# Expert loops of a two-layer gated block: one Sigmoid for SiLU, activations in PSUM, and the next rows converted before the last split

## What is computed

```python
# layer 0: experts with a squared ReLU, F = 256
inter = jnp.einsum('ecd,efd->ecf', binned, w1_stack)
inter = jnp.square(jax.nn.relu(inter))
outb = jnp.einsum('ecf,edf->ecd', inter, w2_stack)
...
# layer 1: experts with SiLU gating, D_FF = 512
g = jnp.einsum('nd,edf->nef', xf, gate_w) + gate_b
u = jnp.einsum('nd,edf->nef', xf, up_w) + up_b
h = jax.nn.silu(g) * u
expert_out = jnp.einsum('nef,efd->ned', h, down_w) + down_b
```

## Time and profile before

| what | before |
|---|---|
| median of 3 runs | 1481.43 us (1478.41 to 1485.65) |
| span of the profiled execution, first to last instruction | 1462.4 us |
| median less that span | 19.0 us |
| PE busy | 1092.1 us, 75% of the span |
| DVE busy | 790.0 us, 54% |
| ACT busy | 418.9 us, 29% |
| POOL busy | 362.7 us, 25% |
| mean granted PE clock | 0.872 of full speed |

### The profile page before, as it was taken

How to read it: one execution, slowest core, us unless ns; L and a number is a source line. 1 busy time by engine, 2 the same in 40 slices (tenths; PEclk the granted TensorE clock), 3 DMA queues, 4 the chain that set the end, 5 groups by cost and what they waited for, 6 DMA issues and landing times.

```text
span 1462.4 us, 16573 instructions
## 1 busy us (share of the span) xinstructions
PE 1092.1 (75%) x5562; PEld 904.4 (62%) x5562; DVE 790.0 (54%) x1774; ACT 418.9 (29%) x788; POOL 362.7 (25%) x294
## 2 busy tenths in 40 slices
PE   1978889787666663998999579898971488897850
PEld 1647666575565662786777458686860377897840
DVE  5456546656444436646565544535455466667633
ACT  1203121122132341233332332424220144453420
POOL 4204152131421351410101220101014322213225
PEclk9989989897888985999999679999985599998985
DMA  7600032000375650200000100000005544443435
GB/s 265 225 1 29 1 119 68 1 0 1 132 212 167 179 174 0 58 0 1 1 0 15 44 29 0 1 0 1 1 1 190 176 130 130 130 137 122 129 99 168
DMA packets 92431, 114.66 MB, mean 78 GB/s; under 512 B 6608, under 2 KB 77776, under 8 KB 92240
## 3 DMA queue, kind: packets, MB, share of 16 engines
q1 hardware_dynamic: 72480, 78.46, 16.5%
q0 software_dynamic: 19888, 35.40, 8.3%
HBM read 77.14 MB, written 36.70 MB: 78 GB/s over the span
## 4 chain that ended last, share of the span: by engine, by line
PE 53%; DVE 22%; issue 6%; POOL 6%; ACT 6%; DMA 5%; SPq 2%; DVEq 0%; POOLq 0%; ACTq 0%
PE PS L194 12%; PE PS L196 11%; PE PS L195 11%; PE PS L1577 7%; PE PS L1493 4%; DVE act L513 3%; PE PS L1468 3%; DMA xg<-routed 3%; POOL routed L759 2%; POOL HB L819 2%; POOL rstd L752 2%; PE PS L1389 1%; PE PS L1516 1%; DVE st L1036 1%; DVE SM L1310 1%
## 5 line engine op out<-in xcount | busy, mean ns | idle before, releaser
L752 POOL TENSOR_TENSOR rstd<-ve,minus_half 128x4 f32<-128x4 f32 x40 | 40.6, 1016 | 410.1 <-DVE ve L1043 251.6
L194 PE MATMUL PS<-xt,split 128*128 128x256 f32 x412 | 121.3, 295 | 10.9 <-issue 7.8
L194 PE MATMUL PS<-split,hs 128*128 128x256 f32 x244 | 84.2, 345 | 49.8 <-DVE hs L521 49.8
L195 PE MATMUL PS<-xt,split 128*128 128x256 f32 x412 | 119.3, 290 | 0.0
L196 PE MATMUL PS<-xt,split 128*128 128x256 f32 x412 | 118.9, 289 | 0.0
L1577 PE MATMUL PS<-VP,HB 128*128 128x257 f32 x384 | 97.0, 416 | 16.0 <-DVE VP L1322 16.0
L1577 PEld LDWEIGHTS PS<-VP,HB 128*128 128x128 f32 x384 | 80.1, 210 | 35.2 <-DVE VP L1322 21.8
L513 DVE SCALAR_TENSOR_TENSOR act<-act 128x256 f32<-128x256 f32 x84 | 70.8, 843 | 56.2 <-ACT act L481 56.2
L446 POOL TENSOR_TENSOR split<-raw,split 128x1024 fp32r<-128x1024 f32 (+1 forms) x15 | 66.5, 4432 | 138.4 <-DMA raw<-down_w 81.9
L194 PEld LDWEIGHTS PS<-xt,split 128*128 128x128 f32 x412 | 82.6, 200 | 14.4 <-issue 10.5
L194 PEld LDWEIGHTS PS<-split,hs 128*128 128x128 f32 x244 | 55.9, 229 | 57.1 <-DVE hs L521 57.1
(11 more groups left out here) (308 smaller groups left out, 2871.4 us busy)
## 6 DMA issues: line engine op xcount, KB each, us to landing
xg<-routed SPq DMA_DIRECT2D x44, 256.0 KB, 2.7
outputs<-y SPq DMA_DIRECT2D x40, 256.0 KB, 3.0
outputs<-zeros SPq DMA_DIRECT2D x3, 2048.0 KB, 16.1
routed<-zeros SPq DMA_DIRECT2D x20, 256.0 KB, 2.5
raw<-m_w SPq DMA_DIRECT2D x16, 256.0 KB, 5.9
split<-m_w POOLq DMA_DIRECT2D x16, 256.0 KB, 4.0
x_base<-X SPq DMA_DIRECT2D x8, 512.0 KB, 3.8
raw<-gate_w SPq DMA_DIRECT2D x8, 512.0 KB, 6.3
```

The costliest lines, as they stand in the source:

```text
L194: pe.matmul(out_, a[1], b[0], start=first, stop=False)
L195: pe.matmul(out_, a[0], b[1], start=False, stop=False)
L752: pool.tensor_tensor(rstd[h][:], ve[h][:], minus_half[:], ALU.pow).then_inc(sem("rstd_ready"), 1)
```

## The change

SiLU is made another way: ACT makes sigmoid(g + gate_b) in one instruction, and DVE makes `(g + gate_b) * sigmoid`, with g read from PSUM. The buffer `hbg` and its one instruction go. `h` is no longer in SBUF: it is written into the PSUM bank of its chunk, columns 256 to 511 (over the up product in stage 1, beside the product in stage 0), and both its parts are made from there. In stage 1 ACT's `x_hi` goes ahead of the last chunk's high part, and DVE's `x_lo` ahead of the last chunk's low part. SP reads the row number of the next load before it waits for the turned rows, and no longer after. The diff, cut:

```diff
         def group_in(sp, m, t):
             r = sp.value_load(table[m][0:1, bass.ds(t + 2 * E, 1)], min_val=0, max_val=XROWS - G)
+            if not isinstance(t, int):
+                counted(sp, m)
+                sp.wait_ge(sem(f"m{m}_turned"), t)
             sp.dma_start(moe[m].xg[:], routed[m][bass.ds(r, G), :].rearrange("(a p) d -> p a d", p=P)).then_inc(sem(f"m{m}_xg"), 16)
...
                 with sp.Fori(lo, hi) as t:
-                    counted(sp, m)
-                    sp.wait_ge(sem(f"m{m}_turned"), t + 2)
                     group_in(sp, m, t + 2)
...
+        def h_part(f):
+            return PS[:, f, G:2 * G]
...
+            def h_hi(t, f):
+                act.wait_ge(sem(f"m{m}_h"), t * w.fc + f + 1)
+                act.activation(w.hs[:, 0, f], h_part(f), ACT.Copy).then_inc(sem(f"m{m}_hhi"), 1)
...
-                            act.activation(w.act[:, f % 2, 0], PS[:, f, 0:G], ACT.Tanh, bias=hbg[:, b:b + 1], scale=0.5)
-                            act.activation(w.act[:, f % 2, 1], PS[:, f, 0:G], ACT.Identity, bias=hbg[:, b:b + 1], scale=0.5).then_inc(sem(f"m{m}_act"), 1)
+                            act.activation(w.act[:, f % 2, 0], PS[:, f, 0:G], ACT.Sigmoid, bias=col("gate_b", b)).then_inc(sem(f"m{m}_act"), 1)
...
+            def h_lo(t, f):
+                dve.wait_ge(sem(f"m{m}_h"), t * w.fc + f + 1)
+                dve.wait_ge(sem(f"m{m}_hhi"), t * w.fc + f + 1)
+                dve.tensor_tensor(w.hs[:, 1, f], h_part(f), w.hs[:, 0, f].bitcast(F32), ALU.subtract).then_inc(sem(f"m{m}_hlo"), 1)
...
-                            dve.scalar_tensor_tensor(out=w.h[:, f], in0=PS[:, f, 0:G], scalar=0.0, in1=a[:, 0],
+                            dve.scalar_tensor_tensor(out=h_part(f), in0=PS[:, f, 0:G], scalar=0.0, in1=a[:, 0],
                                                      op0=ALU.max, op1=ALU.mult).then_inc(sem(f"m{m}_h"), 1)
                         else:
-                            dve.scalar_tensor_tensor(out=a[:, 0], in0=a[:, 0], scalar=1.0, in1=a[:, 1],
-                                                     op0=ALU.add, op1=ALU.mult).then_inc(sem(f"m{m}_silu"), 1)
+                            dve.scalar_tensor_tensor(out=a[:, 1], in0=PS[:, f, 0:G], scalar=col("gate_b", e * w.fc + f),
+                                                     in1=a[:, 0], op0=ALU.add, op1=ALU.mult).then_inc(sem(f"m{m}_silu"), 1)
...
-                            dve.scalar_tensor_tensor(out=w.h[:, f], in0=PS[:, f, G:2 * G], scalar=col("up_b", e * w.fc + f),
-                                                     in1=a[:, 0], op0=ALU.add, op1=ALU.mult).then_inc(sem(f"m{m}_h"), 1)
+                            dve.scalar_tensor_tensor(out=h_part(f), in0=PS[:, f, G:2 * G], scalar=col("up_b", e * w.fc + f),
+                                                     in1=a[:, 1], op0=ALU.add, op1=ALU.mult).then_inc(sem(f"m{m}_h"), 1)
...
+                    if m == 0:
+                        h_lo(t, w.fc - 1)
+                        x_lo(t + 2)
+                    else:
+                        x_lo(t + 2)
+                        h_lo(t, w.fc - 1)
```

More of the change, by code:

```diff
@@ L155, in build @@
         rbf = [sb(f"rbf{h}", [P, 2, TT, E], BF16) for h in two]
-        ONCE = {"act": ("tanh_g", "hbq", "w3_hi", "ew", "gt_hi", "hbg"),
+        ONCE = {"act": ("tanh_g", "hbq", "w3_hi", "ew", "gt_hi"),
                 "dve": ("w3_split", "bb", "g1", "be1", "row_max", "wmax", "ewT", "gt_lo", "gbias"),
@@ L228, in moe_buffers @@
             w.act = sb(f"act{m}", [P, 2, w.ups, G], F32, st)
-            w.h = sb(f"h{m}", [P, w.fc, G], F32, st)
             w.hs = sb(f"hs{m}", [P, 2, w.fc, G], F32R, st)
@@ L269, in build @@
         DB = sb("DB", [P, E, D], F32, part_m[1])
-        hbg = sb("hbg", [P, E * F2 // P], F32, part_m[1])
         part_m[1].close()
@@ L479, in moe_act @@
                             b = e * w.fc + f
-                            act.activation(w.act[:, f % 2, 0], PS[:, f, 0:G], ACT.Tanh, bias=hbg[:, b:b + 1], scale=0.5)
-                            act.activation(w.act[:, f % 2, 1], PS[:, f, 0:G], ACT.Identity, bias=hbg[:, b:b + 1], scale=0.5).then_inc(sem(f"m{m}_act"), 1)
+                            act.activation(w.act[:, f % 2, 0], PS[:, f, 0:G], ACT.Sigmoid, bias=col("gate_b", b)).then_inc(sem(f"m{m}_act"), 1)
                             if f:
-                                act.wait_ge(sem(f"m{m}_h"), t * w.fc + f)
-                                act.activation(w.hs[:, 0, f - 1], w.h[:, f - 1], ACT.Copy).then_inc(sem(f"m{m}_hhi"), 1)
+                                h_hi(t, f - 1)
+                    x_hi(t + 2)
                     if m == 1:
-                        act.wait_ge(sem(f"m{m}_h"), t * w.fc + w.fc)
-                        act.activation(w.hs[:, 0, w.fc - 1], w.h[:, w.fc - 1], ACT.Copy).then_inc(sem(f"m{m}_hhi"), 1)
-                    x_hi(t + 2)
+                        h_hi(t, w.fc - 1)
             if m == 0:
@@ L518, in moe_dve @@
                         if f:
[L519 to L524, removed]
@@ L525, in moe_dve @@
-                    x_lo(t + 2)
+                            h_lo(t, f - 1)
+                    if m == 0:
[4 more added lines that the diff above has]
+                        h_lo(t, w.fc - 1)
                     dve.wait_ge(sem(f"m{m}_down"), t + 1)
@@ L1013, in _ @@
             act.wait_ge(sem("m1_table"), 1)
-            once(act.activation(hbg[:], col("gate_b", 0, E * F2 // P), ACT.Copy, scale=0.5), "hbg")
-            after(act, "hbg")
             moe_act(act, 1)
```

## The result

| what | before | after |
|---|---|---|
| median | 1480.66 us (4 runs, 1478.41 to 1485.65) | 1433.67 us (4 runs, 1428.12 to 1435.82) |
| ratio | | 0.9683, 95% interval 0.9649 to 0.9717 |
| span of the profiled execution | 1462.4 us | 1432.9 us |
| stage m = 1, first up product to last down product | 257.8 us | 215.5 us |
| stage m = 0, the same | 120.9 us | 121.2 us |

What follows compares the result with a forecast made beforehand. DVE was taken to stop for POOL's long subtraction whenever it needs a second SBUF tile, leaving PE waiting. Terms 44.3 + 2.1 + 0.5 - 0.3 = 46.6 us off 1481.4 gave 1434.8 us, range 1426 to 1447.

Steps and rivals of the forecast that it cites:

- (1): Stage 1 loops: with no DVE instruction needing two SBUF tiles, the seven stalls during POOL's subtraction go; 44.3 us gained.
- (2): Stage 1, chain behind a group's last chunk: PE starts that chunk 0.1 us earlier in 21 groups; 2.1 us gained.
- the two signs that would have made the step wrong: Stage 1: PE still standing 0.38 us at its third chunk, or waiting over 0.3 us at the fourth.
- (3): Stage 1, `x_lo` ahead of the last low part: its earlier end gives nothing; the move is counted in (2).
- (4): Writing h to PSUM costs nothing and stage 0 keeps its lengths: 0, between 1 us less and 1 us more.
- (5): SP's load of rows goes out about 0.6 us earlier: 0.5 us gained in stage 0, at most 4.8.
- (6): ACT's one function table load, in the first expert's loop, falls in idle time: 0; uncovered 2.6 us.
- (7): With the stalls gone, PE arrives just as POOL's weights do, at two experts: 0.3 us lost, 2 us at most.
- the sign for a wrong step (7): PE waiting for `split`, the weights POOL prepares, ahead of an expert.
- the rival: Late weights: PE waits at `m1_lo` ahead of two or three experts; 1437 us, or 1444 with slower loads; chance 0.11.
- The lock that stays: DVE stops for POOL at any use of SBUF, or because it writes PSUM: 1479 us; chance 0.03.
- DVE did not become the bound: Rival: PE's writes or ACT's reads hold up DVE in PSUM; 1495 us at 0.30 us longer per instruction; chance 0.02.

Runs made afterwards that it cites:

- second trace of before: The kernel before, run again with no edit for another trace: 1480.07 us, ratio 0.9995, stage 1 260.0 us.
- short_split: The kernel before, with POOL's subtraction of the weights cut to 8 columns for experts 2 to 7 of both stages: 1441.59 us, ratio 0.9731.
- the two halves: The kernel before with only the Sigmoid and new multiply: 1472.11 us, ratio 0.9942; and with only h in PSUM: 1478.33 us, ratio 0.9985.
- old_order: The changed kernel with the last high and low part of h ahead of `x_hi` and `x_lo` again: 1431.48 us, ratio 0.9649.
- old_sp: The changed kernel with SP waiting for the turned rows first and reading the row number after: 1428.87 us, ratio 0.9662.
- split_in_12: The kernel before, with POOL's subtraction in stage 1, experts 1 to 7, in 12 instructions of 256 columns: 1446.02 us, ratio 0.9754.
- raw_on_pool: The changed kernel, with raw weights of experts 2 to 7 loaded from POOL's queue behind its subtraction instead of from SP's: 1418.52 us, ratio 0.9566.

## Why the prediction was right, and where not

**(1) The stall: right in kind and size.** Stage 1 went from 257.8 to 215.5, 42.3 us less. By the steps it should have been 44.3 from the stalls and 2.1 from the chain, less the late weights, which cost 3.9: 42.5. Against the second trace of before it is 44.5, so an agreement within 0.2 says no more than that the sum is right within some 2 us. Short_split gives 6.2 to 6.6 us a stall by itself, without any of the change. The reading that it takes a second tile from SBUF is shown by the two halves: each frees just the instruction that it gives a PSUM operand, and the other one takes over the stall.

**The total: closer than its terms.** Forecast were 46.6 us, measured 47.0. Stage 1 gave 42.3 to 44.5 of them, stage 0 nothing against the first trace, and the other 2.5 to 4.7 us are in no step of the prediction; between executions of one kernel the parts outside of stage 1 differ by more than that. That the sum meets the median within half a microsecond is luck.

**(2) The chain: right, and for the reason given.** S is the start of ACT's first instruction for the last chunk. I had the last low part start at S + 2.35 and be done at 2.77, and PE begin the last chunk at 2.83. With S = 1201.96 it starts at 1204.32, S + 2.36, and PE begins at 1204.79, S + 2.83. A middle group without a stall took 9.70 before (short_split, and 9.70 also from 1280.36 in the first trace) and takes 9.60, 0.10 less; the first group of an expert went from 9.79 to 9.69. Neither of the two signs that would have made the step wrong is in the trace. What I did not draw from my own numbers is (3).

**(3) `x_lo` ahead of the last low part: missed.** The prediction said that its earlier end gives nothing, which holds, and left the cost inside (2), where it can't be seen. Without `x_lo` in front the last low part starts at S + 2.04 (old_order), and not at S + 2.36. The Sigmoid form alone saves 0.3 us a group, and the moved `x_lo` gives back 0.2 of it.

**(4) h in PSUM: right.** The low part takes 414 ns from PSUM, against 415 from SBUF. The 65 ns that the prediction estimated from the table of the Trainium skill ("VectorE: DVE Perf Modes", the TRN2 errata) for a PSUM source do not appear in this form, which takes its other tile from SBUF. The product that also writes to PSUM takes 493 ns, 9 more than L516; in stage 0 it is 433 against 424. ACT's Copy for the high part gains, 378 ns from PSUM against 416 from SBUF. And "stage 0 keeps its lengths" overlooks one thing: in the second trace of before, two low parts of stage 0 with both inputs in SBUF took 1.77 and 1.50 us instead of 0.42, at 510.34 and 512.03; POOL worked on SBUF tiles beside both, with its subtraction of 1024 columns (2.35 us from 509.48) and an instruction behind it (1.46 us from 511.79). The first trace has no such case, and the changed kernel has none.

**(5) SP: 0.5 forecast, nothing seen** (old_sp), and 0.5 us is too little for these runs to show.

**(6) The function table: right.** Two loads of 1283 ns, one for each group of the first expert, both in ACT's idle time: the second ends at 1175.39 and the Sigmoid begins at 1177.44.

**(7) Late weights: right place, wrong price.** I took 0.3 us and 2 at most. It was one expert, and 3.9 us, so the sign for a wrong step (7) is there, two groups lie well outside the lengths that I gave, and the stage has 215.5 us instead of 211. I had held the end of POOL's subtraction against the end of PE's groups. But PE's first matmul comes 1.8 us after that end (1.5 in old_order and old_sp), where a usual turn costs 0.7, and the subtraction ended 21.0 us after the high parts were asked for, not 19.7. These two make the 2.4 us of waiting; why the loads took longer is open. The fall of the granted clock, which I had written down for the rival and not for this step, added 1.5. It does not always come: in old_order PE stood idle 2.48 us ahead of one expert and its next group ran at a granted clock of 1.00 in 9.49 us, and 2.36 us ahead of the following one, where the next group had 0.84 and took 10.97; in old_sp it stayed at 1.00 behind both waits. Old_order, old_sp and split_in_12 show the same wait, at one or two experts, and raw_on_pool takes it away.

**What lies around the span.** I put 19.0 us there. It is 1.7 to 1.8 us; the other 17 belong to an execution that was shorter than all of the measured runs. The forecast came out since the sum was taken off the median. Had I added it up from spans, as I did for "a span of about 1416", I would have been wrong by 17 us, and that number was: it is 1432.9.

**The rivals.** The lock that stays would have left 6 us instructions, and there are none, though DVE now writes to PSUM beside POOL. Late weights came at one expert, where the rival had two or three, and cost 3.6 us more than stands in the sum. DVE did not become the bound: its three instructions of a chunk kept to 484, 493 and 414 ns beside PE's writes and ACT's reads.

## What to carry to other kernels

Look at the longest duration of a DVE line beside its median. Where it is many times as long and begins inside a POOL instruction, count the tiles that it reads from SBUF: give every such instruction in the queue one operand from PSUM, since one that is left keeps the loss, or cut POOL's instruction into pieces, which needs no other edit and gave three quarters here. Then look at what the stalls had covered: weights that arrived just in time were late afterwards, and it took an earlier load before the order on DVE showed in the time.

## What the runs showed that I had not expected

Twelve pieces of 256 columns cost POOL more than one of 3072: its 84 instructions in stage 1 are busy for 67.4 us, so 9.6 us a subtraction against 6.7. How much of that is DVE's turns and how much the cutting, no run separates. Still the group lost only 0.9 us. POOL in turn was hardly held up by DVE's instructions with one SBUF tile: 6.78 to 6.85 us with DVE working inside, against 6.70 to 6.93 with DVE standing.
